# Later layers of two graphs in flight over 29 slots, four graphs to a loop body, four residual additions on TensorE

## The chip, the cores and the metric

The kernel runs on one core of one Trainium2 chip. The metric is the device time of one execution in microseconds. Three runs of the kernel before give a median of 3404.64 us, from 3402.95 to 3406.09.

Engines are named as in the profile: PE (TensorE, matmuls) with PEld (its weight loads), DVE (VectorE), ACT (ScalarE), POOL (GpSimd) and SP (SyncE, which issues every DMA here).

## What is computed

64 graphs of 128 nodes with 128 features go through four graph layers, each followed by a residual and a normalisation. All of it is fp32. Per graph, with `x` and `adj` 128 x 128:

```python
# layer 0: every pair of nodes
h = relu((x @ W1[:H])[:, None] + (x @ W1[H:])[None, :] + b1)   # 128*128 rows of 128
y = layernorm(h @ W2 + b2) * gamma + beta
x = norm(x + einsum('ij,ijh->ih', adj, y))
# layer 1: degree-normalised product, weights, relu; layer 2: two-layer MLP with a node mask
x = norm(x + relu(adj_norm @ x @ W.T + b))
x = norm(x + mask * (relu(((1 + eps) * x + adj.T @ x) @ W1 + b1) @ W2 + b2))
# layer 3: three times
for i in range(3):
    h = relu(layernorm(adj.T @ (h @ Ws[i]) + bs[i] + h) * gammas[i] + betas[i])
x = norm(x + h)
```

Layer 0 is nearly all the arithmetic: 16384 rows per graph. The rest, here called the tail, is a long chain of single 128 x 128 steps.

## The kernel before, in words

A graph's pairs are cut into 16 slots of 8 units (a unit is one node against all 128, a 128 x 128 tile). For slot `t` of a graph:

- `hidden` (DVE L610, ACT L507) makes `h[:, t]` from `uT` and `vT`: DVE 3 units in even slots and 2 in odd ones (`vector_units`), ACT the others. Slots 0 to 13 on ACT read the PSUM copy `v_ps`, 14 and 15 the SBUF copy `vT`.
- `products` (PE L369) multiplies two blocks of 512 columns by `w2c` into one of two PSUM buffers `y_ps`.
- `squares` (ACT L517) squares them into a ring of four, `variances` (PE L381) sums the squares over two slots.
- Each half graph (8 slots), `deviations` (ACT L524) takes the root, SP moves it into another layout (`straighten_deviations`), DVE inverts (L632) and multiplies by the adjacency to the coefficients `c` (L640). SP stores `c` to DRAM and reads it back to all partitions, four broadcasts of 1 MB per half graph (`spread_coefficients`, L305, into `cb`).
- `weighted_sum` (DVE L624) multiplies `h` by `cb` and sums into a column of `gT`: 8 per slot, 128 per graph.

The engines run the same software pipeline, written by hand. An iteration starts one graph and has 16 slots on each engine; a stage of a graph lags by a number of slots: hidden units by START = 4, products by 5, squares by 6, weighted sums by TTR_LAG = 19, the tail by TAIL_LAG = 33. `lagging` turns a lag into a graph and a slot. Each engine's queue is in order, so the order of the work is the order of the program.

The table `AT` gives each tail step a slot and one of FINE = 9 steps in it; on DVE step `k` follows weighted sum `k`. The tail takes 15 slots, so one graph's is in flight at a time, in single buffers. PE does tail steps 0 to 3 between its two products and the others after them; ACT does them between Square and hidden units.

A normalisation is `bn_stats` (L648), `bn_aggr` one step later (L651), two operations on POOL (L848, L850), and NORM_AT = 4 steps after the statistics the scaling on DVE (L657). In layer 3 the residual is added by DVE (L718) from PSUM into `z`, from which statistics and scaling read; layer 0's is L692.

`program` writes out iterations 0 to 3, then a hardware loop `Fori(4, 63)` whose body is one iteration, then four more that drain the pipeline. Inside the loop, waits compare with values worked out from the loop's register.

PE turns `x` of the next graph at slot 14 (`turn_x`, into `turn_bank`), ACT keeps it at the end of slot 15 (`keep_xT`, L489), PE makes `u` and `v` at slot 3 (`make_uv`), ACT keeps them at the end of slot 3 (`keep_uv`, L496 and L497), once per graph. SP's order in an iteration: spread of the first half, output store, `x_in` load, second half's deviations, coefficients and spread, the adjacency load of 8 DMAs, first half's deviations and coefficients, and `load_tail`.

## Time and profile before

| | |
|---|---|
| median of three runs | 3404.64 us |
| profiled execution's own time | 3402.17 us |
| its span, first to last instruction | 3400.4 us |
| PE busy | 2933.5 us (86%), 10882 instructions |
| DVE busy | 2919.2 us (86%), 21905 |
| ACT busy | 2821.7 us (83%), 7620 |
| POOL busy | 403.7 us (12%), 978 |
| mean granted TensorE clock | 0.945 |
| instruction fetch (queue q14) | 318 packets, 2.61 MB |
| chain that ended last | DVE 29%, PE 24%, "issue" 17%, ACT 14% of the span |

"Busy" is the time in which an engine executes something; register, branch, semaphore and DMA-issuing instructions are not in it. "Idle before, releaser" of a row is the time the engine stood before that instruction, and what ended it; "issue" means that nothing the profile shows was waited for. A matmul of fp32 appears as two instructions. The ends of matmuls are modelled, so starts are the safer numbers.

### The profile page before, as it was taken

The page shows a single profiled execution, that of the slowest core. Times are in us where ns is not written, and L with a number is a line of the kernel's source. Part 1 is how long each engine was busy: PE and PEld are TensorE (multiplying, and loading weights), DVE is VectorE, ACT ScalarE, POOL GpSimd, SP SyncE. Part 2 cuts the span into 40 slices and gives each one's busy share as a digit, 9 for nine tenths or more (in the row PEclk, how much of TensorE's full clock was granted, in tenths as well). Part 3 has the DMA queues.
Part 4 walks back from the last instruction along what each step waited for, and adds up shares of the span by engine and source line. Part 5 has one row for each costly group of instructions (what it writes and reads, how often), then busy time and mean ns, then how long its engine had stood idle before and what let it go on. Part 6 is the DMA issues. An engine that isn't in the chain of part 4 may idle for free.

```text
span 3400.4 us, 69689 instructions
## 1 busy us (share of the span) xinstructions
PE 2933.5 (86%) x10882; PEld 1150.1 (34%) x10882; DVE 2919.2 (86%) x21905; ACT 2821.7 (83%) x7620; POOL 403.7 (12%) x978
## 2 busy tenths in 40 slices
PE   8988888888888888888888888888888888888894
PEld 2333333333333333333333333333333333333332
DVE  5988888888888888888888888888888888888896
ACT  8988888888888888888888888888888888888892
POOL 0111111111111111111111111111111111111111
PEclk9999999999999999999999999999999999999996
DMA  3544444444444444444444344444444444434442
GB/s 123 208 159 174 182 167 156 169 191 162 158 171 183 169 156 159 196 167 158 158 181 184 156 159 185 179 159 157 175 190 156 159 175 183 164 156 167 192 162 106
DMA packets 170182, 570.56 MB, mean 168 GB/s; under 512 B 68608, under 2 KB 104320, under 8 KB 104320
## 3 DMA queue, kind: packets, MB, share of 16 engines
q1 hardware_dynamic: 169856, 567.82, 42.8%
q14 instruction: 318, 2.61, 0.2%
q8 instruction: 8, 0.13, 0.0%
HBM read 555.17 MB, written 8.39 MB: 166 GB/s over the span
## 4 chain that ended last, share of the span: by engine, by line
DVE 29%; PE 24%; issue 17%; ACT 14%; SPq 5%; DMA 5%; POOL 4%; DVEq 1%; ACTq 0%; POOLq 0%
PE y_ps L369 14%; DVE h L624 13%; ACT h L507 8%; PE ss_ps L381 6%; DVE h L610 5%; DMA devs<-dev_rows 5%; SPq L286 5%; POOL rs L850 3%; ACT sq L517 2%; DVE gT L624 2%; PE prod_bank L432 2%; ACT dev_rows L524 2%; DVE stats L648 2%; ACT h L555 1%; DVE x L657 1%
## 5 line engine op out<-in xcount | busy, mean ns | idle before, releaser
L369 PE MATMUL y_ps<-h,w2c 128*128 128x512 f32 x4096 | 2152.3, 637 | 209.7 <-DVE h L610 207.1
L624 DVE CUSTOM_DVE_ANT_0 h<-h,cb 128x128 f32<-128x128 f32 x8192 | 1953.1, 283 | 9.4 <-DMA cb<-c_scratch 0.4
L507 ACT ACTIVATE h<-uv_ps,uT 128x128 f32<-128x128 f32 x4928 | 1429.6, 400 | 235.5 <-DVE gT L624 230.3
L517 ACT ACTIVATE sq<-y_ps,b2c_col 128x1024 f32<-128x1024 f32 x1024 | 1164.1, 1137 | 143.8 <-PE y_ps L369 134.9
L369 PEld LDWEIGHTS y_ps<-h,w2c 128*128 128x128 f32 x4096 | 694.7, 196 | 1091.2 <-issue 934.0
L610 DVE TENSOR_SCALAR h<-vT,uT 128x128 f32<-128x128 f32 x2560 | 591.8, 282 | 188.6 <-issue 158.8
L624 DVE DVE_READ_ACCUMULATOR2_ANT gT<- 128x1 f32 x8192 | 670.8, 82 | 0.1
L381 PE MATMUL ss_ps<-sq,sel 128*32 128x512 f32 x4096 | 581.4, 642 | 0.5 <-ACT sq L517 0.5
L848 POOL TENSOR_TENSOR var_eps<-mv,eps_col 128x1 f32<-128x1 f32 x448 | 84.8, 189 | 2657.3 <-DVE mv L651 2657.3
L850 POOL TENSOR_TENSOR rs<-var_eps,minus_half 128x1 f32<-128x1 f32 x448 | 277.0, 618 | 35.1
L507 ACT ACTIVATE h<-vT,uT 128x128 f32<-128x128 f32 x704 | 219.4, 400 | 0.0
L381 PEld LDWEIGHTS ss_ps<-sq,sel 128*32 128x32 f32 x4096 | 82.8, 111 | 351.2 <-issue 297.5
L657 DVE TENSOR_SCALAR x<-z,mv,rs 128x128 f32<-128x128 f32 x256 | 88.7, 346 | 93.3 <-POOL rs L850 91.0
L648 DVE BATCH_NORM_STATS2 stats<-z 128x6 f32<-128x128 f32 x448 | 129.5, 289 | 0.2
L432 PE MATMUL prod_bank<-adj_in,h 128*128 128x128 f32 x256 | 63.7, 331 | 69.2 <-ACT h L555 69.2
L632 DVE RECIPROCAL invs<-devs 128x64 f32<-128x64 f32 x128 | 70.6, 552 | 51.9 <-DMA devs<-dev_rows 47.8
L432 PE MATMUL prod_bank<-adj_in,x 128*128 128x128 f32 x128 | 31.9, 331 | 79.3 <-DVE x L657 79.3
L432 PEld LDWEIGHTS prod_bank<-adj_in,h 128*128 128x128 f32 x256 | 38.9, 191 | 173.4 <-ACT h L555 173.4
L436 PEld LDWEIGHTS prod_bank<-l3w,aggT 128*128 128x128 f32 x384 | 68.9, 194 | 81.4 <-issue 77.4
L555 ACT ACTIVATE h<-z_aff 128x128 f32<-128x128 f32 x192 | 59.5, 310 | 40.5 <-DVE z_aff L731 38.6
L420 PE MATMUL prod_bank<-adj_in,x 128*128 128x128 f32 x128 | 31.9, 331 | 64.0 <-DVE x L657 64.0
L524 ACT ACTIVATE dev_rows<-ss_ps 128x512 f32<-128x512 f32 x128 | 82.6, 645 | 1.2 <-PE ss_ps L381 1.2
(99 smaller groups left out, 1556.2 us busy)
## 6 DMA issues: line engine op xcount, KB each, us to landing
cb<-c_scratch SPq DMA_DIRECT2D x512, 1024.0 KB, 8.1
adj_c<-in_adj_dram SPq DMA_DIRECT2D x512, 8.0 KB
devs<-dev_rows SPq DMA_DIRECT2D x512, 8.0 KB
x_in<-in_x_dram SPq DMA_DIRECT2D x64, 64.0 KB, 9.5
c_scratch<-c SPq DMA_DIRECT2D x128, 32.0 KB, 1.4
adj_in<-in_adj_dram SPq DMA_DIRECT2D x64, 64.0 KB, 2.0
x_res<-in_x_dram SPq DMA_DIRECT2D x64, 64.0 KB, 1.9
out_dram<-x SPq DMA_DIRECT2D x64, 64.0 KB, 10.1
```

The costliest lines, as they stand in the source:

```text
L286: sp.dma_start(devs[32 * p:32 * p + 32, half, :], dev_rows[p:P:32, half, :].rearrange("q (r j) -> q r j", j=SPAN)).then_inc(devs_in[half], 16)
L369: op = pe.matmul(y_ps[:, t % 2, c0:c0 + COLS], w2c[:], h[:, t, c0:c0 + COLS], start=True, stop=True)
L381: mm = pe.matmul(ss_ps[32 * q:32 * q + 32, :], sel[:, ROWS - 1 - p:ROWS - 1 - p + 32], sq[:, (t + q // 2) % SQ_RING, c0:c0 + COLS], start= ...
L432: pe.matmul(prod, (x3 if i == 0 else h3)[:], adj_in[:], start=True, stop=True).then_inc(l3_agged[i], 1)
L507: op = act.activation(h[:, t, n * P:(n + 1) * P], v, ACT.Relu, bias=uT[:, i:i + 1])
L517: act.activation(sq[:, t % SQ_RING, :], y_ps[:, t % 2, :], ACT.Square, bias=b2c_col[:], scale=float(P) ** -0.5).then_inc(sq_done, 1)
L524: act.activation(dev_rows[:, half, :], ss_ps[:], ACT.Sqrt, bias=EPS).then_inc(dev_done, 1)
L610: op = dve.tensor_scalar(h[:, t, n * P:(n + 1) * P], vT[:], uT[:, i:i + 1], 0.0, ALU.add, ALU.max)
L624: op = dve.tensor_tensor_reduce(h[:, t, cols], h[:, t, cols], cb[:, t // 2, c0:c0 + P], 1.0, 0.0, ALU.mult, ALU.add, gT[:, i:i + 1])
L648: dve.bn_stats(stats[:], z[:]).then_inc(stats_set[name], 1)
L657: dve.tensor_scalar(dst[:], z[:], mv[:, 0:1], rs[:], ALU.subtract, ALU.mult).then_inc(normed[name], 1)
L850: pool.tensor_tensor(rs[:], var_eps[:], minus_half[:], ALU.pow).then_inc(rs_set[name], 1)
```

## The change

- **Two tails in flight.** The tail's steps are placed over 29 slots (the last, `ln3`, at slot 28). `tails` gives two graphs with their buffers to every engine at every slot, one in its first 16 slots, one in its last. All tail tensors get a second buffer, and there are two PSUM product banks; the bank of the transposes goes, its parts move into `prod_bank` and `uv_ps`.
- **Four graphs to a loop body** (UNROLL): seven iterations are written out, 56 are done in 14 rounds of four, and four drain.
- **Four residual additions** (`l0_sum` and `l3_sum0` to `2`) become a third product into the same PSUM sum, identity by residual. `bn_stats`, layer 3's first scaling (`z_aff`) and layer 0's normalisation then read PSUM.
- NORM_AT is 7 for both scalings. `norm`'s order is otherwise the same.
- **DVE makes 2 hidden units in every slot**, ACT 6. `uT` and `vT` have two buffers. ACT reads `v_ps` up to slot 12 (SPLIT_AT).
- Weighted sums and tail start one slot earlier (18 and 32). DVE does its hidden units after the first weighted sum of a slot.
- The transpose of `x` moves to slot 1, `make_uv` to slot 2, `keep_xT` to the end of slot 1, `keep_uv` into slot 3 behind the Square. SP loads the tail after the adjacency and stores the output after that.

```diff
-TTR_LAG = START + 15
-TAIL_LAG = START + 29
+TTR_LAG = START + 14
+TAIL_LAG = START + 28
+UNROLL = 4
+SPLIT_AT = 13
-NORM_AT, AFFINE_AT = 4, 5
+NORM_AT = 7
-def vector_units(t):
-    return 3 if t % 2 == 0 else 2
+VECTOR_UNITS = 2
...
+    ("g_keep", 2, 0), ("l0_mm", 3, 0), ("ln0", 3, 4), ("x1_scaled", 4, 5),
...
+    ("l3_agg0", 12, 4), ("l3_agg_keep0", 13, 2), ("l3_mm0", 13, 4),     ("l3_ln0", 14, 3), ("l3_relu0", 16, 2), ("l3_agg1", 19, 0), ("l3_agg_keep1", 19, 8),
...
-            for i in range(4):
-                iteration(i + 1, (i, *(i - d if i >= d else None for d in range(1, 4))))
-            with eng.Fori(4, G - 1) as g:
-                iteration(g + 1, (g, g - 1, g - 2, g - 3))
+            first = 4 + (G - 5) % UNROLL
+            for i in range(first):
+                iteration(i + 1, about(i), i % 2)
+            with eng.Fori(0, (G - 1 - first) // UNROLL) as rounds:
+                for n in range(UNROLL):
+                    g = UNROLL * rounds + (first + n)
+                    iteration(g + 1, (g, g - 1, g - 2, g - 3), (first + n) % 2)
...
+        def tails(graphs, buf, s):
+
+            return [(graphs[d], (buf - d) % 2, (s + SLOTS * (d - 2)) * FINE) for d in (2, 3)]
...
-                    pe.matmul(prod, gT_keep[:], w2cg[:], start=True, stop=False)
-                    pe.matmul(prod, adjT[:], beta0[:], start=False, stop=True).then_inc(l0_made, 1)
+                    pe.matmul(out, gT_keep[:, b, :], w2cg[:], start=True, stop=False)
+                    pe.matmul(out, adjT[:, b, :], beta0[:], start=False, stop=False)
+                    pe.matmul(out, ident[:], x_base[:, b, :], start=False, stop=True).then_inc(l0_made, 1)
...
+                        pe.matmul(out, aggT[:, b, :], l3w[:, i, :], start=True, stop=False)
+                        pe.matmul(out, ident[:], (x3 if i == 0 else h3)[:, b, :], start=False, stop=False)
+                        pe.matmul(out, pick[:], bias_parts[:, 1 + i, :], start=False, stop=True
...
+                    if s == 1 and new is not None:
+                        turn_x(new)
+                    if s == 2 and new is not None:
+                        make_uv(new)
...
-                    for n in range(first, DUO_UNITS):
-                        if n == first + 2:
-                            later_layers(g, place + 4, place + 6)
+                    for n in range(VECTOR_UNITS, DUO_UNITS):
+                        if n == VECTOR_UNITS + 2:
+                            tail_steps(4, 6)
...
+                    if s == 1 and new is not None:
+                        keep_xT(new)
...
-                    if due(f"l3_sum{i}"):
-                        wait(dve, l3_made[i], g + 1)
-                        dve.tensor_tensor(z[:], prod, (x3 if i == 0 else h3)[:], ALU.add).then_inc(z_set[name], 1)
...
-                    hidden_step = BLOCK_UNITS if ht == 0 else 0
+                    hidden_step = BLOCK_UNITS if ht == 0 else 0 if t == 0 else 1
```

## Rows read from the trace of the kernel before

**Rows 1.** All executions of line L497: count, duration min/median/max, first and last start.
```profile
L497 ACT ACTIVATE vT<-uv_ps x64: 267/268/271, 11.0 to 3281.4; 128x128 f32<-128x128 f32 x64
```

**Rows 2.** Timeline of ACT, L497 of graphs 3 and 4: start, duration.
```profile
142.62 0.27 ACT L497 ACTIVATE vT<-uv_ps 128x128 f32<-128x128 f32 x1
...
190.88 0.27 ACT L497 ACTIVATE vT<-uv_ps 128x128 f32<-128x128 f32 x1
```

**Rows 3.** Busy by stretch: length, PE, PEld, DVE, ACT, POOL, PEclk, DMA share, GB/s.
```profile
53.60:95.60 42.00, 40.33 (x142) 12.77 (x140) 38.41 (x307) 41.37 (x111) 0.85 (x3) 1.00 0.52 203
...
142.90:191.20 48.30, 43.80 (x174) 17.07 (x170) 45.18 (x344) 43.95 (x120) 6.13 (x15) 1.00 0.46 182
191.20:243.70 52.50, 45.54 (x178) 17.77 (x170) 45.88 (x346) 44.09 (x120) 6.20 (x15) 0.97 0.47 184
```

**Rows 4.** Waits from 243.7 to 3281: us in total, times, longest.
```profile
ACT h L507 <- DVE gT L624: 224.0, 80, 4.1
...
DVE h L610 <- issue: 156.0, 57, 2.9
...
ACT sq L517 <- PE y_ps L369: 127.3, 194, 2.3
...
DVE x L657 <- POOL rs L850: 79.8, 174, 0.5
...
ACT aggT L542 <- PE prod_bank L421: 66.0, 58, 1.4
DVE z L718 <- PE prod_bank L437: 60.2, 174, 0.5
```

**Rows 5.** Timeline over one end of the loop's body: start, duration, [idle before].
```profile
1644.62 1.14 ACT L517 ACTIVATE sq<-y_ps,b2c_col 128x1024 f32<-128x1024 f32 x1
...
1648.89 0.68 DVE L610 TENSOR_SCALAR h<-vT,uT 128x128 f32<-128x128 f32 x3 [2.80 <-issue]
...
1649.69 1.65 PE L369 MATMUL y_ps<-h,w2c 128*128 128x512 f32 x2 [3.50 <-DVE h L610]
...
1652.23 1.14 ACT L507 ACTIVATE h<-uv_ps,uT 128x128 f32<-128x128 f32 x4 [3.91 <-DVE gT L624]
```

**Rows 6.** Timeline of ACT in a stretch where it is the bound.
```profile
51.08 1.85 ACT L507 ACTIVATE h<-vT,uT 128x128 f32<-128x128 f32 x6
...
55.71 1.17 ACT L517 ACTIVATE sq<-y_ps,b2c_col 128x1024 f32<-128x1024 f32 x1
56.70 1.72 ACT L507 ACTIVATE h<-uv_ps,uT 128x128 f32<-128x128 f32 x6
58.20 1.23 ACT L517 ACTIVATE sq<-y_ps,b2c_col 128x1024 f32<-128x1024 f32 x1
```

**Rows 7.** Groups by line: count | busy us, mean ns | idle before.
```profile
L610 DVE TENSOR_SCALAR h<-vT,uT 128x128 f32<-128x128 f32 x2560 | 591.8, 282 | 188.6 <-issue 158.8 <-ACT vT L497 4.0 <-ACT mask_all L562 3.1
...
L731 DVE SCALAR_TENSOR_TENSOR z_aff<-z_aff,rs,l3beta 128x128 f32<-128x128 f32 x192 | 66.7, 347 | 2.6 <-POOL rs L850 2.6
...
L718 DVE TENSOR_TENSOR z<-prod_bank,h 128x128 f32<-128x128 f32 x128 | 37.3, 291 | 37.5 <-PE prod_bank L437 37.5
...
L701 DVE SCALAR_TENSOR_TENSOR z_aff<-prod_bank,dis,l1b 128x128 f32<-128x128 f32 x64 | 22.2, 347 | 2.0 <-PE prod_bank L417 2.0
```

**Rows 8.** Timeline of PE, an identity product and the product behind it.
```profile
152.34 0.39 PE L421 MATMUL prod_bank<-ident_eps,x 128*128 128x128 f32 x2
152.56 1.02 PE L369 MATMUL y_ps<-h,w2c 128*128 128x512 f32 x2
```

**Rows 9.** Timeline of DVE and SP, from the coefficients to their broadcast.
```profile
1645.02 0.23 DVE L640 CUSTOM_DVE_ANT_0 c<-adj_c,invs 128x64 f32<-128x64 f32 x1
...
1647.68 2.00 SPq L305 DMA_DIRECT2D cb<-c_scratch  x4
```

**Rows 10.** Tile `cb` from 1590 to 1660, twelve broadcasts of 1 MB.
```profile
DMA to landing us min/median/max: 4.4/7.8/12.2
```

**Rows 11.** Line L688 from 3300 to 3401, the last two graphs.
```profile
L688 DVE COPY gT_keep<-gT x2: 221/224/226, 3327.5 to 3367.6; 128x128 f32<-128x128 f32 x2
```

More of the change, by code:

```diff
@@ L333, in iteration @@
                         load_adj_c(new)
+                    load_tail(old, 1 - buf)
+                if oldest is not None:
+                    wait_apart(sp, normed["ln3"], oldest + 1)
+                    wait_apart(sp, out_stored, 16 * oldest)
+                    sp.dma_start(out[oldest], x4[:, 1 - buf, :]).then_inc(out_stored, 16)
                 if new is not None:
@@ L336, in iteration @@
                     store_coefficients(new, 0)
-                if old is not None:
-                    load_tail(old)
             program(sp, iteration)
@@ L347, in turn_x @@
                 wait(pe, x_in_in, 16 * (g + 1))
-                wait(pe, adjT_set, g - 2)
-                wait(pe, xT_set, g)
+                wait(pe, uv_ready, g)
+                wait(pe, h_act, SLOTS * (g - 1) + SPLIT_AT)
                 pe.transpose(xturn_ps, x_in[:], ident[:]).then_inc(x_turned, 1)
@@ L459, in _, with iteration @@
             pe.wait_ge(set_up, 1)
-            def iteration(after, graphs):
+            def iteration(after, graphs, buf):
                 new = graphs[0]
@@ L559, in later_set_up, with iteration @@
                 act.wait_ge(wT_turned, 1)
-                act.activation(l1wT[:], prod, ACT.Copy).then_inc(wT_set, 1)
+                act.activation(l1wT[:], prod[0], ACT.Copy).then_inc(wT_set, 1)
                 act.wait_ge(mask_turned, 1)
-                act.activation(mask_all[:], turn_ps[:, 0:G], ACT.Copy).then_inc(mask_set, 1)
+                act.activation(mask_all[:], prod[1][:, 0:G], ACT.Copy).then_inc(mask_set, 1)
             act.wait_ge(weights_in, 16 * WEIGHTS)
-            keep_xT(0)
             act.wait_ge(b2c_set, 1)
-            def iteration(after, graphs):
+            def iteration(after, graphs, buf):
                 new = graphs[0]
@@ L686, in later_layers @@
                     wait(dve, ttr_done, SLOTS * (g + 1))
-                    wait(dve, l0_made, g)
-                    dve.tensor_copy(gT_keep[:], gT[:]).then_inc(g_kept, 1)
-                if due("l0_sum"):
-                    wait(dve, l0_made, g + 1)
-                    wait(dve, x_base_set, g + 1)
-                    dve.tensor_tensor(z[:], prod, x_base[:], ALU.add).then_inc(z_set["ln0"], 1)
-                norm(g, "ln0", x1, lo, hi)
+                    wait(dve, l0_made, g - 1)
+                    dve.tensor_copy(gT_keep[:, b, :], gT[:]).then_inc(g_kept, 1)
+                norm(g, b, "ln0", x1, lo, hi)
                 if due("x1_scaled"):
@@ L778, in later_set_up, with iteration @@
                 dve.wait_ge(affine_set, 2)
-            def iteration(after, graphs):
+            def iteration(after, graphs, buf):
                 new = graphs[0]
@@ L792, in iteration @@
                             if hg is not None:
-                                for n in range(vector_units(ht)):
-                                    hidden(hg, ht, n)
+                                for n in range(VECTOR_UNITS):
+                                    hidden(hg, hb, ht, n)
                         elif wg is not None:
                             weighted_sum(wg, t, k - (k > hidden_step))
-                        later_layers(g, place * FINE + k, place * FINE + k + 1)
+                        for g, b, place in tails(graphs, buf, s):
+                            later_layers(g, b, place + k, place + k + 1)
                         if ct % HALF == 0 and cg is not None and k == 5:
@@ L847, in later_layers, with iteration @@
                         wait(pool, mv_set[name], g + 1)
[L848 removed]
+                        pool.tensor_tensor(var_eps[:, b:b + 1], mv[:, b, 1:2], eps_col[:], ALU.add
+                                           ).then_inc(eps_added[name], 1)
                         wait(pool, eps_added[name], g + 1)
[L850 removed]
+                        pool.tensor_tensor(rs[:, b:b + 1], var_eps[:, b:b + 1], minus_half[:], ALU.pow
+                                           ).then_inc(rs_set[name], 1)
             pool.wait_ge(ones_set, 5)
[L854 removed]
+            def iteration(after, graphs, buf):
                 for s in range(SLOTS):
[L856 to L857 removed]
+                    for k in range(FINE):
+                        for g, b, place in tails(graphs, buf, s):
+                            later_layers(g, b, place + k, place + k + 1)
             program(pool, iteration)
```

272 lines of the change are left out of this document (131 added, 141 removed), and 15 rows, old and new, of the table AT.

## Prediction, made before the changed kernel was run

> **What bounds the kernel now.** I read the views in this order: the whole iterations, the waits of the loop, one passage over the end of the loop body, the pitch of single instructions.
>
> First the length of an iteration. ACT's copy of `vT` (L497) runs once per graph and marks time. Graph 3's starts at 142.62 and graph 4's at 190.88: 48.26 us, in the last iteration written out ahead of the loop, with the pipeline full. Graph 63's starts at 3281.4, so the 59 iterations in the loop took (3281.4 - 190.88) / 59 = 52.38 us each [rows 1, 2]. The loop body has the same work and costs 4.12 us more, 243 us in all.
>
> Then who is full. In the written-out iteration DVE is busy for 45.18 us, ACT 43.95, PE 43.80. DVE is the first bound and the others are close. In the iteration from 53.6 to 95.6, before any tail runs, ACT is busy for 41.37 of 42.00 us, 98.5%: ACT as the bound leaves almost no gap [rows 3].
>
> Then the loop's 4.12 us. Of the waits inside it, DVE's hidden unit waits 156.0 us for "issue", 57 times: 2.74 us once per iteration. The passage over the body's end shows it: DVE starts L610 at 1648.89 after 2.80 us of nothing, PE after 3.50 us (for that DVE result), ACT later still, 3.91 us for `gT`. ACT's own turn into the next iteration, the Square at 1644.62, has no gap listed before it: ACT wrapped round at no cost and stood only because DVE did [rows 4, 5]. Behind the gap PE runs two products in 1.65 us, against 1.02 elsewhere; the granted clock is 1.00 in the written-out iteration and 0.97 in the first looped one [rows 3, 5, 8]. So an end of the body costs 2.74 us of fetch on DVE and some 1.4 us behind it.
>
> **The change, part by part, per full iteration.**
>
> Four graphs to a body. The first seven iterations are written out, 56 stay in the loop: 14 rounds, 13 jumps back instead of 58. At (243 / 58) = 4.19 us a jump, 45 fewer give -189 us. The cover of the 13 that stay goes down: ACT will have no spare time (below), so I keep the full 4.19.
>
> The rule of the Trainium skill that bears on this is in "Runtime: NRT & Kernel Launch", section "Instruction fetch mechanics": a taken branch to a target outside the two held blocks (512 instructions, 2048 on PE) forces a fetch before execution goes on. The trace agrees as far as DVE stalls and ACT, with a third of the instructions, does not. By that rule the fourfold bodies of ACT, SyncE and GpSimd no longer fit either, which is a rival below.
>
> Hidden units. DVE makes 2 of 8 in each slot, not 3 and 2 by turns: 8 units move to ACT. On ACT a slot of Square and six hidden units is 58.20 - 55.71 = 2.49 us, the six being (58.20 - 56.70) / 6 = 0.25 each: +2.0 us. Six more units read `vT` in SBUF (SPLIT_AT 13 instead of 14); six from there take 1.85 us against 1.72, so +0.1 [rows 6]. ACT: 43.95 + 2.1 = 46.1 us busy. DVE loses 8 x 0.231 (591.8 / 2560) = 1.85 us [rows 7].
>
> Four residual additions. DVE loses four of 0.29 us (37.3 / 128) = 1.2 us, 0.8 if their overlap with neighbours is left out; I take 1.0. PE gains four fp32 identity products; the one that exists, L421, starts at 152.34 and the next product at 152.56: 0.22 each, +0.9 us, of which no part is the bound. Statistics and scaling now read PSUM. An operation that does so already, L701, takes 347 ns, the same form from SBUF, L731, 347: nothing, at most 0.07 x 9 = 0.6 us on DVE if each were worse by a fifth, none of it on the path while DVE has the room below [rows 7, 8].
>
> Sums per full iteration: ACT 46.1, PE 43.8 + 0.9 = 44.7, DVE 45.2 - 1.85 - 1.0 = 42.3.
>
> Waits. A tail that takes 29 slots gives each step about twice the distance to its source. In the loop that can free DVE of POOL's `rs` (79.8 us, 1.4 per iteration) and of PE's product (60.2, 1.0), and ACT of PE (L542: 66.0, 1.1) [rows 4]. I do not add these, since the sum is made from ACT's busy time. NORM_AT 7 puts six weighted sums ahead of the normalisation, so DVE no longer stands there. What is late next is ACT itself: it is in order, and Square, hidden units and tail steps fill it. New waits: `keep_xT` now ends ACT's slot 1 and needs PE's transpose from the same slot; behind it on ACT stands the next Square, which PE's next but one product needs. Ahead of that transpose PE has two products of 1.02 us [rows 8] and the small ones of c_sum, some 2.5 us of a 2.9 us slot, so I price it at 0 to 0.5 us. On the SyncE queue the `x_in` load waits for that same transpose ahead of `straighten_deviations(old, 1)`; that one is due at slot 6, so nothing. The store of the output has moved behind the tail's loads and is ready by slot 13, one slot before the deviations behind it: nothing.
>
> The length: ACT 46.1 at 98.5% gives 46.8; with the `keep_xT` wait and a PE at 95% beside it I take 47.0 (bounds 46.1 and 48.3). That is 48.3 - 47.0 = 1.3 us less per iteration.
>
> Weighted sums one slot earlier. The broadcast of coefficients has one slot less. `c` is made at 1645.02, its spread issued at 1647.68, and the first landing is 4.4 us after issue at best: 1652.1, 7.1 us after `c` [rows 9, 10]. From slot 15, step 6, to slot 18 are 2.3 slots of 2.94 us = 6.8 us. So DVE may stand for 0.3 us, twice per iteration, in a spare of 47.0 - 42.3 = 4.7 us: nothing in the sum. In exchange ACT's hidden units come two slots behind the sums that free `h`, which is the wait of 224.0 us of the loop [rows 4].
>
> Fill and drain. Iterations 0 and 1 are ACT's: +2 us each; 2 and 3 gain 1.3 each: +1.4. At the end the last `gT_keep` starts at 3367.6 and the span ends at 3400.4 [rows 11]: 32.8 us of pure chain, in which four additions (4 x 0.29) leave and four products at half clock (4 x 0.44) come; graph 62's second half now runs beside it in the same in-order queues. I take +3 (bounds 0 and +10).
>
> **Sum.** Against the profiled execution's 3402.17: -189 - 59 x 1.3 (77) + 1.4 + 3 = 3140.6. The median of the runs is 2.5 us above that execution: 3143.
>
> **Rivals.**
>
> (a) The loop's extra time is not the jump alone. If only 2.74 us belong to the jump and the other 1.45 us to each looped iteration (waits on register values, which every looped iteration keeps), then (45 - 3) x 1.45 = 61 us don't go: 3204. For it: a wait in the loop compares with a value worked out from the loop's register, in a written-out iteration with a constant. Against it: behind the gap PE is visibly slow, and ACT's longest waits for `gT` stand there [rows 4, 5]. Chance 0.18.
>
> (b) PE and ACT hold each other. PE at 44.7 and ACT at 46.1 share two y buffers; in the loop ACT's Square already waits 127.3 us for PE [rows 4]. If their jitter costs what DVE's relief gives, the iteration stays at 48.3: 3143 + 77 = 3220. Against it: those waits fall mostly behind the gap, and the iteration at 98.5% had the same buffers. Chance 0.17.
>
> (c) Every engine fetches at the jump. ACT's own 2.8 us come on top of the DVE chain, 13 x 2.8 = 36: 3179. This is what the rule named above would add, if the engines' fetches do not overlap. Chance 0.15, within reach of the forecast.
>
> (d) ACT runs without a gap at 46.1 and a jump costs only DVE's 2.74 us: -53 - 19: 3071. Chance 0.07.
>
> (e) Slower. The broadcast decides. If with the earlier sums each half comes as late as its slowest landing (12.2 us instead of 4.4, [rows 10]), DVE stands 8.1 us twice, 16.2 less the spare 4.7: +11.5 per iteration, 3143 + 63 x 11.5 = 3870. It beats the 259 us gained from 4.4 us per full iteration on, that is when each half is late by some 4.5 us. Against it: the later landings belong to later pieces, each needed two slots after the one before. Chance 0.03.
>
> **How the numbers follow.** The forecast, 3143 (3110 to 3175 by its own bounds), has 0.39. It is the likeliest, so it is the number. For 8 in 10 the range takes in (a), (b) and (c) and reaches two thirds of the way to (d): 3090 to 3235. The last 0.01 is for an outcome near no change. A difference from no change can be told for this kernel from about 0.2%, 7 us. Faster by more than that: 0.96; within it 0.01; slower 0.03.
>
> **What would show it.** Right: `vT` copies in the loop about 47 us apart with one of about 51 in four; DVE's "issue" wait 13 times, not 57; ACT busy for over 93% of the middle; DVE with idle time of 3 to 5 us per iteration, mostly at the reciprocal and the first weighted sums. (a): evenly 48.4 in the loop's straight parts, with ACT below 96% busy. (b): ACT's Square waiting for PE for over 1 us per iteration. (c): an "issue" wait on ACT. (e): L624 waiting for the DMA of `cb`. Wrong altogether if written-out iterations come to more than 48.3 us.

## The result, and the profile after

The changed kernel takes 3042.06 us, the median of four runs from 3027.88 to 3046.78. Beside it on the same chip the kernel before takes 3405.36. The ratio is 0.8925, 95% interval 0.8894 to 0.8956: 363 us less, where 262 were forecast, and below the range's lower end of 3090. The profiled execution of after took 3046.78 us, its span is 3045.0.

The lines of the page of after that matter: span, busy time by engine, the granted clock in 40 slices, instruction fetch, the chain that ended last, and ACT's two large groups.

```profile
span 3045.0 us, 67885 instructions
...
PE 2900.1 (95%) x11394; PEld 1178.0 (39%) x11394; DVE 2679.4 (88%) x21137; ACT 2883.4 (95%) x8132; POOL 424.1 (14%) x978
...
PEclk9999999999999999999999999999999999999996
...
q14 instruction: 408, 3.34, 0.3%
...
ACT 67%; issue 14%; PE 8%; DMA 7%; DVE 2%; SPq 2%; ACTq 0%; POOL 0%; DVEq 0%; POOLq 0%
...
L512 ACT ACTIVATE h<-uv_ps,uT 128x128 f32<-128x128 f32 x4992 | 1739.5, 776 | 0.0
...
L522 ACT ACTIVATE sq<-y_ps,b2c_col 128x1024 f32<-128x1024 f32 x1024 | 1560.1, 1524 | 29.6 <-PE y_ps L375 29.5
```

ACT holds 67% of the chain, and the pieces of 0.2 to 1.0 us that the chain calls "issue" between 2470 and 2530 us all lie between two instructions of ACT, not at a jump. One group to note: a hidden unit on ACT has a mean of 776 ns and a Square 1524. The same Square took 1.17 and 1.23 us where ACT stood now and then [rows 6]. That has to do with the error of the forecast.

Then three iterations in a row inside the loop: two undisturbed ones and one that holds a jump back. Columns: stretch, length, PE, PEld, DVE, ACT and POOL busy, PEclk, DMA share, GB/s. They answer to [rows 3].

```profile
2424.48:2469.07 44.59, 44.17 (x178) 17.63 (x177) 41.67 (x329) 44.59 (x129) 6.32 (x15) 1.00 0.50 198
2469.07:2513.94 44.87, 44.32 (x180) 17.91 (x180) 41.18 (x327) 44.87 (x129) 6.61 (x15) 1.00 0.50 194
2513.94:2566.36 52.42, 48.56 (x178) 19.49 (x178) 43.46 (x344) 45.76 (x130) 6.56 (x15) 0.90 0.54 212
```

The first two take 44.6 and 44.9 us with ACT busy throughout, and so do those written out ahead of the loop (44.86 or 44.87 for graphs 3 to 5); that an iteration waits on a loop's register makes no difference. The one with the jump takes 52.42, at a mean clock of 0.90. The iteration right behind a jump, not shown, takes 45.8 on average.

The 13 iterations with a jump have not one price: four take 49.0 to 49.5 us at a mean clock of 0.965, eight 52.0 to 52.8 at 0.902, and the first 55.0 at 0.907. DVE stands 2.7 to 3.0 us in both kinds, PE 3.3 to 3.8 in the first and 3.3 to 4.5 in the second; what differs is how much of the iteration PE runs at the lower clock.

The waits of after (us in total, times, longest), against [rows 4]:

```profile
DVE invs L639 <- DMA devs<-dev_rows: 126.1, 108, 26.8
DVE h L631 <- DMA cb<-c_scratch: 107.5, 113, 3.6
PE y_ps L375 <- DVE h L617: 73.0, 69, 4.5
ACT xT L494 <- PE uv_ps L358: 55.5, 13, 5.4
DVE h L631 <- issue: 36.6, 13, 3.0
...
ACT sq L522 <- PE y_ps L375: 29.5, 27, 2.2
```

ACT's wait for `gT` (224.0 before) is gone and its wait for PE is 29.5 instead of 127.3. DVE stops for "issue" 13 times instead of 57, 2.8 us each. In its place come a wait of ACT for PE's transpose, 4.3 us 13 times, and DVE's waits for transfers, which lie in the time that DVE has spare.

**Where the 94 us between forecast (3140.6) and the profiled execution are.** `vT` of graph 4 starts at 187.39, that of graph 63 at 2930.93: 2743.5 us for 59 iterations.

| Term | forecast | measured | difference |
|---|---|---|---|
| undisturbed iteration, x59 | 47.0 | 44.87 | -126 |
| 13 jumps | 54.5 | 2743.5 - 59 x 44.87 = 96 (7.4 each) | +42 |
| up to graph 4 | 190.88 + 1.4 = 192.3 | 187.39 | -5 |
| behind graph 63's `vT` | 119.0 + 3 = 122 | 3045.0 - 2930.93 = 114.1 | -8 |

That is -97; the other 3 us are the rounding of 48.26 to 48.3 in the forecast's gain of 1.3 per iteration. Two terms have to be explained, an iteration that is shorter and a jump that is dearer, and they have opposite signs.

### The profile page after: what moved, and what is told of

The parts are those of the page before. It is cut to its first block, busy times and chain, and to the rows that moved or that the text cites. A ratio compares the mean times of both kernels' runs of the same rounds, so it can differ in the third digit from the quotient of the medians.

```text
span 3045.0 us, 67885 instructions
## 1 busy us (share of the span) xinstructions
PE 2900.1 (95%) x11394; PEld 1178.0 (39%) x11394; DVE 2679.4 (88%) x21137; ACT 2883.4 (95%) x8132; POOL 424.1 (14%) x978
## 4 chain that ended last, share of the span: by engine, by line
ACT 67%; issue 14%; PE 8%; DMA 7%; DVE 2%; SPq 2%; ACTq 0%; POOL 0%; DVEq 0%; POOLq 0%
ACT h L512 37%; ACT sq L522 22%; PE y_ps L375 5%; DMA cb<-c_scratch 3%; ACT dev_rows L529 2%; ACT aggT L555 2%; DMA devs<-dev_rows 2%; SPq L295 2%; PE ss_ps L387 1%; ACT aggT L547 1%; DMA c_scratch<-c 1%; DVE h L631 1%; ACT h L560 0%; ACTq L208 0%; ACT xT L494 0%
## 5 line engine op out<-in xcount | busy, mean ns | idle before, releaser
L631 DVE CUSTOM_DVE_ANT_0 h<-h,cb 128x128 f32<-128x128 f32 x8192 | 1936.8, 281 | 146.2 <-DMA cb<-c_scratch 107.5
L512 ACT ACTIVATE h<-uv_ps,uT 128x128 f32<-128x128 f32 x4992 | 1739.5, 776 | 0.0
L522 ACT ACTIVATE sq<-y_ps,b2c_col 128x1024 f32<-128x1024 f32 x1024 | 1560.1, 1524 | 29.6 <-PE y_ps L375 29.5
L617 DVE TENSOR_SCALAR h<-vT,uT 128x128 f32<-128x128 f32 x2048 | 485.6, 279 | 8.3 <-ACT vT L502 4.3
L512 ACT ACTIVATE h<-vT,uT 128x128 f32<-128x128 f32 x1152 | 446.0, 870 | 0.0
L560 ACT ACTIVATE h<-z_aff 128x128 f32<-128x128 f32 x192 | 129.4, 674 | 27.8 <-DVE z_aff L742 27.6
L555 ACT ACTIVATE aggT<-prod_bank 128x128 f32<-128x128 f32 x192 | 134.0, 698 | 19.7 <-PE prod_bank L436 19.7
L665 DVE BATCH_NORM_STATS2 stats<-prod_bank 128x6 f32<-128x128 f32 x256 | 74.8, 292 | 41.4 <-PE prod_bank L415 34.9
L494 ACT ACTIVATE xT<-uv_ps 128x128 f32<-128x128 f32 x64 | 45.0, 703 | 55.5 <-PE uv_ps L358 55.5
L440 PE MATMUL prod_bank<-l3w,aggT 128*128 128x128 f32 x384 | 81.1, 294 | 4.2 <-ACT aggT L555 2.6
L668 DVE BATCH_NORM_AGGREGATE mv<-stats 128x2 f32<-128x6 f32 x448 | 78.3, 175 | 0.3
```

The source lines that it names most:

```text
L440: pe.matmul(out, aggT[:, b, :], l3w[:, i, :], start=True, stop=False)
L512: op = act.activation(h[:, t, n * P:(n + 1) * P], v, ACT.Relu, bias=uT[:, b, i:i + 1])
L522: act.activation(sq[:, t % SQ_RING, :], y_ps[:, t % 2, :], ACT.Square, bias=b2c_col[:], scale=float(P) ** -0.5).then_inc(sq_done, 1)
L555: act.activation(aggT[:, b, :], prod[b], ACT.Copy).then_inc(l3_agg_kept[i], 1)
L560: act.activation(h3[:, b, :], z_aff[:, b, :], ACT.Relu).then_inc(l3_relued[i], 1)
L617: op = dve.tensor_scalar(h[:, t, n * P:(n + 1) * P], vT[:, b, :], uT[:, b, i:i + 1], 0.0, ALU.add, ALU.max)
```

## The experiments

Theory A: ACT is the bound of an undisturbed iteration, and its iteration is the sum of the distances from start to start of its instructions, not of their durations. A jump costs DVE's fetch and, behind it, PE at half clock, which ACT then waits for. Rival B: the iteration is held by the coupling of PE and ACT over two `y` buffers, so that work taken off ACT brings nothing. Rival C: the extra time of the loop is not the jump alone.

Results in one table; "from" is the kernel that was edited. "Iteration" is the mean from one `vT` copy to the next between graphs 4 and 63, those with a jump left out; "with a jump" is the mean of these. In the text an undisturbed iteration is the usual one, 44.87 us in after and e1; their means are higher by some longer ones. The runs stand on several chips, on which the kernel before took from 3402.89 to 3408.47 us, so differences between runs of different chips are good to some 5 us.

| Run | from | median us | ratio to before (95%) | iteration | with a jump |
|---|---|---|---|---|---|
| after | | 3042.06 | 0.8925 (0.8894 to 0.8956) | 45.07 | 51.57 |
| e1_all_written_out | after | 2958.06 | 0.8691 (0.8676 to 0.8705) | 44.95 | |
| e2_two_to_a_body | after | 3139.89 | 0.9222 (0.9203 to 0.9241) | 45.66 | 50.95 |
| e4_adds_on_dve | after | 3022.65 | 0.8892 (0.8862 to 0.8922) | 45.12 | 49.65 |
| e8_pe_kept_busy | after | 2998.62 | 0.8811 (0.8796 to 0.8826) | 45.06 | 47.86 |
| e3_units_3_2 | after | 3015.94 | 0.8871 (0.8846 to 0.8897) | 44.99 | 49.59 |
| e7_out_units_2_1 | e1 | 3086.94 | 0.9069 (0.9051 to 0.9087) | 47.06 | |
| e5_out_units_3_2 | e1 | 2929.01 | 0.8594 (0.8578 to 0.8610) | 44.61 | |
| e12_out_units_3_every_4 | e1 | 2914.12 | 0.8551 (0.8536 to 0.8565) | 44.33 | |
| e11_out_keep_same_slot | e1 | 2953.19 | 0.8666 (0.8651 to 0.8680) | 44.89 | |
| e14_out_chain_in_one_slot | e1 | 3012.99 | 0.8851 (0.8836 to 0.8866) | 45.85 | |
| e6_before_four | before | 3270.44 | 0.9599 (0.9583 to 0.9615) | 48.45 | 56.31 |
| e13_before_four_padded | e6 | 3229.54 | 0.9486 (0.9470 to 0.9502) | 48.42 | 53.25 |
| e9_before_written_out | before | 3152.48 | 0.9261 (0.9243 to 0.9280) | 48.13 | |
| e10_before_out_units_2 | e9 | 3091.04 | 0.9081 (0.9063 to 0.9099) | 47.09 | |

### What a jump costs

**No jump at all.**

```diff
-            first = 4 + (G - 5) % UNROLL
-            for i in range(first):
+            for i in range(G - 1):
                 iteration(i + 1, about(i), i % 2)
-            with eng.Fori(0, (G - 1 - first) // UNROLL) as rounds:
-                for n in range(UNROLL):
...
```

> The changed kernel with all 67 iterations written out, no loop and no jump; everything else as it is. In the changed kernel the iterations inside a round take 44.6 to 45.9 us between two vT copies and the one over a jump up to 52.4. Theory A (a jump costs 7.4 us in all: 2.8 of fetch on VectorE, the rest in TensorE at half its clock behind the gap): 13 jumps go, 3042 - 96 = 2946 us, and the granted clock comes to 1.00 outside fill and drain. Rival B (a jump costs the 4.19 us of the prediction and the rest of the loop's excess has another cause): 2988. Rival C (looped iterations are dear because their waits use register values): every one of 56 iterations gains, and the written-out kernel's iterations come out shorter than the 44.86 us of graphs 3 to 6.

2958.06, 84 us less than after: 84 / 13 = 6.5 us a jump (7.4 in the slower profiled execution). It lies between A's 2946 and B's 2988, nearer to A. The undisturbed iteration stays at 44.87, so looped iterations are not dear by themselves.

**Twice as many jumps**: `UNROLL = 2`, 28 jumps.

> The changed kernel with two graphs to a body instead of four: 5 iterations written out, 29 rounds, 28 jumps instead of 13. Theory A (7.4 us a jump): 3042 + 15 x 7.4 = 3153 us. Rival B (4.19 us a jump, as in the prediction): 3105. Rival D (a smaller body is fetched in less time or not at all on ACT, PE and SyncE): under 3080.

3139.89: (3139.89 - 3042.06) / 15 = 6.5 us for each added jump, between A's 7.4 and B's 4.19. That this equals the 6.5 of after is not a law of the jump: this body stops DVE twice per jump, 2.8 us and, starting 0.9 us later, 4.1, together 6.9 instead of 2.8. So part of the two stops must be covered; how much each costs was not isolated. The waits (us in total, times, longest):

```profile
DVE gT L631 <- issue: 116.1, 28, 4.6
...
DVE h L631 <- issue: 78.9, 28, 3.0
```

**Inside one jump of after** (start, duration, idle before). DVE stops 2.79 us; PE then takes 3.77 and 3.48 us for two slots' products. A product of 512 columns appears as two instructions, so each `x4` is two products, at some 1.8 us each against 1.02 [rows 8]. ACT stands twice behind PE.

```profile
2366.47 0.29 DVE L631 CUSTOM_DVE_ANT_0 h<-h,cb 128x128 f32<-128x128 f32 x1 [2.79 <-issue]
...
2367.29 3.77 PE L375 MATMUL y_ps<-h,w2c 128*128 128x512 f32 x4 [3.54 <-DVE h L617]
...
2371.57 0.45 PE L358 MATMUL uv_ps<-ident,x_in 128*128 128x128 f32 x1
...
2372.14 0.28 ACT L494 ACTIVATE xT<-uv_ps 128x128 f32<-128x128 f32 x1 [4.40 <-PE uv_ps L358]
...
2373.82 3.48 PE L375 MATMUL y_ps<-h,w2c 128*128 128x512 f32 x4
...
2377.34 1.11 ACT L522 ACTIVATE sq<-y_ps,b2c_col 128x1024 f32<-128x1024 f32 x1 [2.17 <-PE y_ps L375]
```

The stretch in numbers, columns as above; the granted clock is 0.53, the 1.2 GHz level nearly throughout, where the 10 us before it had 1.00. PE had just stood for 3.54 us.

```profile
2366.00:2376.00 10.00, 8.71 (x20) 3.73 (x21) 8.61 (x70) 4.77 (x15) 0.66 (x1) 0.53 0.86 336
```

The transpose that ACT's `keep_xT` waits for stands behind two products at that clock. ACT's two stops at this jump come to 4.40 + 2.17 = 6.6 us; the mean cost of a jump in this execution is 7.4.

**PE kept at work over DVE's stop.** Four products whose result is overwritten, ahead of the first real one of each body, on an `h` slot that has long been made (work added, outputs unchanged).

```diff
+                    if s == 0 and at_jump[0]:
+                        wait(pe, sq_done, SLOTS * yg + t - 1)
+                        for _ in range(4):
+                            pe.matmul(y_ps[:, t % 2, 0:COLS], w2c[:], h[:, t - 1, 0:COLS], start=True, stop=True)
```

> The changed kernel with four extra products of 512 columns (about 3.6 us) on PE at the head of each round of the loop, into the y buffer that the next product overwrites: they fill the gap in which PE waits for VectorE after the jump. They add work and no result. Theory A (some 4 of a jump's 7 us are PE at half its clock behind the gap): the granted clock stays at 1.00 over the jump, the iteration over a jump falls from 49 to 52 to about 48, and the time by 13 x 3.5 = 45 us: 2997. Rival B (the clock is a symptom, what costs is the order of the queues): 3042 within 10. Rival C (the extra products only delay PE): 13 x 3.6 = 47 us slower, 3089.

2998.62, 43 us less than after, as A expected (2997). Each iteration with a jump takes 47.9 instead of 49.0 to 55.0. The four extra products are the eight instructions of the first line, and the real one behind them (two instructions) runs at full speed:

```profile
498.46 3.70 PE L478 MATMUL y_ps<-h,w2c 128*128 128x512 f32 x8
502.00 1.02 PE L379 MATMUL y_ps<-h,w2c 128*128 128x512 f32 x2
```

ACT's wait for the transpose of `x` is gone from the waits (one for that of `adj`, 29.6 us in 14, stands there instead), and DVE's stop is as it was, 35.5 us in 13. So of 84 us of jumps half (43) is PE's clock, and the other 41 (3.1 per jump) is what DVE's stop of 2.8 costs with PE at full speed.

**The four additions back on DVE.**

```diff
-                    pe.matmul(out, ident[:], x_base[:, b, :], start=False, stop=True).then_inc(l0_made, 1)
...
+                    dve.tensor_tensor(z[:, b, :], prod[b], x_base[:, b, :], ALU.add).then_inc(z_set[name], 1)
...
-                        pe.matmul(out, ident[:], (x3 if i == 0 else h3)[:, b, :], start=False, stop=False)
...
+                    dve.tensor_tensor(z[:, b, :], prod[b], res[:, b, :], ALU.add).then_inc(z_set[name], 1)
```

> The changed kernel with the four residual additions back on VectorE, right ahead of the statistics, without the identity products. Theory A (ACT sets the iteration, VectorE has 3 us of room and PE some): nothing, 3042 within 10 us, and the span of an undisturbed iteration stays at 44.86. Rival B (PE is the bound beside ACT): 4 x 0.22 us less on PE, 59 x 0.9 = 53 us faster, 2990. Rival C (VectorE's work stands in a path): 4 x 0.2 us more, 3090.

3022.65, 19 us less than after and outside A's 10, though the two intervals (0.8862 to 0.8922, 0.8894 to 0.8956) overlap. The iterations without a jump are the same, 45.1 on average in both. So the identity products, which the change names, bring nothing here: DVE, which they relieve, isn't the bound. The 19 us lie in the jumps: 11 of 13 at 48.9 to 49.5 us (clock 0.965) and two at 52.2 (0.902), where the profiled execution of after has four and eight (and the 55.0). But each kernel also has a run of the other kind: after one of 3027.88 us at a clock of 0.979, e4 one of 3040.14 at 0.974. So it isn't shown that the four products per graph on PE make a jump dearer; which of the two prices a jump gets varies from run to run.

### What bounds the undisturbed iteration

**One unit in two slots taken from DVE and given to ACT** (from e1; ACT +8 units per graph), and **one in two slots given back to DVE**, written out and in the loop.

```diff
-VECTOR_UNITS = 2
+def vector_units(t):
+    return 2 if t % 2 == 0 else 1      # e7;  3 and 2 in e5 and e3
```

> The changed kernel, written out, with VectorE making 2 and 1 hidden units by turns: 8 units per graph more on ACT. The written-out changed kernel takes 2958 us and 44.97 per iteration. Theory A (ACT is the bound by the pitch of its instructions, 0.25 us a unit): +2.0 per graph, 2958 + 63 x 2.0 = 3084 us. Rival B (ACT still has room behind PE): under 3050. Rival C (units from ACT's queue delay PE as well): over 3110.

3086.94, and the undisturbed iteration goes from 44.87 to 46.99: +2.1 for eight units of 0.25. ACT is the bound, with no slack at all.

> The changed kernel, written out, with 3 and 2 hidden units on VectorE by turns. Written out it takes 2958 us; in the loop the same edit of the units gave 26 us. Theory A (the three engines are then equally full, 43.3 to 43.6 us of 44.7 busy, and their jitter eats most of it): 44.5 per iteration, 2935. Rival B (the 26 us came from the jumps, where ACT has less to catch up): 2955 or more. Rival C (ACT was the only bound and the jumps hid the gain): 2958 - 63 x 1.6 = 2857.

2929.01, 0.3 us less per iteration, from 44.95 on average to 44.6, where 2 us were taken off ACT. Now no engine is the bound alone. Written out, the stretch from 200 to 2800 of e1, then of e5:

```profile
200.00:2800.00 2600.00, 2562.24 (x10298) 1040.82 (x10295) 2400.28 (x19094) 2596.29 (x7346) 381.66 (x866) 1.00 0.51 199
```

```profile
200.00:2800.00 2600.00, 2523.42 (x10368) 1067.16 (x10367) 2504.01 (x19702) 2518.76 (x6938) 382.90 (x876) 1.00 0.52 200
```

ACT goes from 99.9% to 96.9%, DVE from 92.3 to 96.3, PE from 98.5 to 97.1: three engines within a per cent of each other, none full.

The timelines of ACT tell more than the busy shares. Give each instruction the distance to the next start that it has in e1's unbroken stretches: Square 1.00, a unit 0.25 from PSUM and 0.29 from SBUF, `dev_rows` 0.48, a copy 0.16, `hid` and `uT` 0.25, a relu 0.20. What an iteration takes above that sum is ACT waiting, listed as idle or not (means over 56 iterations):

| Run | iteration | sum of distances | above it | of this ahead of Squares |
|---|---|---|---|---|
| e7 | 47.06 | 46.10 | 0.96 | 0.62 |
| e1 | 44.96 | 44.02 | 0.94 | 0.51 |
| e12 | 44.33 | 43.02 | 1.31 | 0.74 |
| e5 | 44.61 | 41.97 | 2.64 | 1.72 |

With 1.5 and 2 units on DVE the iteration is ACT's sum and an unchanged 0.95; with 2.5 the Squares wait for PE. So B's coupling exists, but as the next limit behind ACT's.

> The changed kernel with VectorE making 3 and 2 hidden units by turns again, so ACT has 8 units of 0.25 us less per graph. Theory A (ACT alone sets the 44.86 us of an undisturbed iteration, by the pitch of its instructions): the iteration falls towards the next engine, VectorE at 41.5 + 1.85 = 43.3 us busy: 43.4 to 43.9, time 2960 to 2990. Rival B (PE, 44.3 us busy of 44.7, is as much the bound): the iteration stays above 44.5, 3020 to 3045. Rival C (VectorE's delays at the coefficients then decide): slower, above 3050.

3015.94, 26 us less than after, where A expected 52 to 82: nearer to B. In the loop the gain lies elsewhere than in e5: the iterations without a jump take 44.99 on average, after's 45.07, and those with one 49.6 instead of 51.6. As with e4, part of that may be which price the jumps got in this execution.

**Three units in every fourth slot** (from e1: `return 3 if t % 4 == 0 else 2`).

> The changed kernel, written out, with 3 hidden units on VectorE in every fourth slot and 2 in the others: 4 units per graph from ACT to VectorE. Theory A (ACT is the bound until about 44.4 us): 4 x 0.25 = 1.0 off until the others bind, 44.3 per iteration: 2920 to 2935, at or under the version with 3 and 2 by turns. Rival B (what that version gains is all there is, in proportion): 2945.

2914.12, below A's 2920 to 2935, with an iteration of 44.3 us: the best of all, 128 us below after and 491 below before. Of the four splits tried, 1.5, 2, 2.25 and 2.5 units, the third is the best.

### What the staging over 29 slots brings

**The old kernel written out, then with 2 units per slot.** e9 replaces the loop of before by 63 iterations in a row; e10 also has `vector_units` return 2.

> The kernel before with all its iterations written out and nothing else changed. Its last written-out iteration took 48.26 us against 52.38 in the loop. Theory A (the whole excess of 4.1 us belongs to the jump): 190.9 + 59 x 48.3 + 119 + 2 = 3160 us, 245 less than before. Rival B (some of the excess belongs to the jump only, and late iterations have another load than the fourth): 3200 or more.

3152.48, a little under A's 3160, beside 3402.89 for before on that chip: 250.4 / 58 = 4.32 us a jump, against the 4.19 that the prediction read from the trace.

> The kernel before, written out, with VectorE making 2 hidden units in every slot, so 8 units per graph move to ACT; one tail at a time and the additions on VectorE as before. Theory A (VectorE, its work and its 2.9 us of waits for POOL and PE, sets the 48.3 us; ACT's pitch comes to 44.9): 48.3 - 1.85 = 46.4, which is 118 us under the written-out kernel before: about 3040. Rival B (ACT already the bound at 46.8, as the prediction had it): 3070. Rival C (the waits of the tail vanish once VectorE has room, so that two tails in flight bring nothing): 44.9 per iteration, 2960.

3091.04, an iteration of 47.07: every expectation was missed. With the units shared as in e1, the old staging, and whatever else the change moves, costs 2.1 us more per iteration. The waits of e10 from 200 to 2800 show ACT late at one copy per graph and at one Square, and DVE at three sums:

```profile
DVE z L716 <- PE prod_bank L435: 89.4, 165, 0.7
...
ACT aggT L540 <- PE prod_bank L419: 37.7, 56, 0.7
...
ACT sq L515 <- PE y_ps L367: 22.5, 55, 0.5
```

Their listed part on ACT is (37.7 + 22.5) / 55 = 1.1 us. The rest lies under the overlap of ACT's records, and the distances from start to start show it: e10's iteration of 47.08 is a sum of 43.76 and 3.32 above it, e1's 44.02 and 0.94. So the whole 2.1 us is ACT coming late to work that others have to finish first: in e10 1.0 ahead of Squares, 0.9 at that copy, 0.6 ahead of hidden units, 0.3 at the relus, 0.3 at `uT` and 0.2 at the other copy. Which part of the change (two tails, `make_uv` earlier, the weighted sums' lag) removes which was isolated for the copy alone, below.

**Part of the old closeness put back into the new kernel** (from e1): each step one slot or less behind its source.

```diff
-NORM_AT = 7
+NORM_AT = 4
...
-    ("ln1", 7, 2), ("l2_agg", 8, 4), ("l2_agg_keep", 9, 2),
+    ("ln1", 8, 0), ("l2_agg", 8, 4), ("l2_agg_keep", 8, 8),
```

> The changed kernel, written out (2958 us), with layer 1's normalisation, layer 2's product and its copy on ACT in one slot as in the kernel before: NORM_AT 4, ln1 at (8, 0), the copy at (8, 8). Theory A (what two tails bring to an ACT-bound iteration is that no source is late for ACT; in the kernel before with 2 units these waits add up to 2.1 us per graph, 0.8 of it at this copy): +0.8 per graph, 3010 us, with a wait of ACT for PE at the copy of about 0.7 us. Rival B (the distance within the slot is enough, and the 2.1 us come from the single buffers and the lag of the weighted sums): under 2970, no such wait.

3012.99, as A expected (3010): +0.95 us per iteration. On ACT a single listed wait comes with it, the copy of the aggregate behind PE, 57 times between 200 and 2800 us:

```profile
ACT aggT L542 <- PE prod_bank L420: 54.6, 57, 1.3
```

The copy moved alone, e11 (`("l2_agg_keep", 8, 8)` and no more), costs nothing: 2953.19, as B expected.

> The changed kernel, written out, with one tail step of ACT back in the place it had: the copy of layer 2's aggregate at the end of the slot of its product (8, 8) instead of one slot later (9, 2). Theory A (what two tails in flight bring is the distance of ACT's steps from their sources: in the kernel before with 2 units, this copy waits 0.68 us per graph by the profile and some 0.15 more under the end of the instruction before it): +0.8 per graph, 2958 + 50 = 3008 us. Rival B (ACT makes it up elsewhere): 2958 within 8.

So the distance to a source counts only as a whole: with step, normalisation and copy in one slot ACT is late by 1 us; with the normalisation earlier no wait at the copy is listed. (e14's `NORM_AT` of 4 holds for every normalisation; on DVE it brings waits for POOL, 118.8 us in 256 at `x`, in time that DVE has spare.)

### The old kernel's jumps, four times fewer

**Four iterations to a body in the kernel before**, nothing else.

```diff
-            with eng.Fori(4, G - 1) as g:
-                iteration(g + 1, (g, g - 1, g - 2, g - 3))
+            with eng.Fori(0, 14) as rounds:
+                for n in range(4):
+                    g = 4 * rounds + (7 + n)
+                    iteration(g + 1, (g, g - 1, g - 2, g - 3))
```

> The kernel before with four graphs to a loop body and nothing else of the change: 7 iterations written out, 13 jumps instead of 58. The kernel before takes 3404 us in the loop and 3152 written out, 252 / 58 = 4.34 us a jump. Theory A (a jump of the old schedule costs the same at 13 as at 58): 3152 + 13 x 4.34 = 3209 us; the prediction's own term (189 less) says 3215. Rival B (a jump of the fourfold body costs the 6.5 us that it costs in the changed kernel, because now PE, ACT and SyncE fetch too): 3152 + 85 = 3237.

3270.44: 135 us less than before where 196 (A) or 168 (B) was expected, so neither holds: (3270.4 - 3152.5) / 13 = 9.1 us a jump. DVE stops twice, 2.55 us apart, and PE stands 6.63 us:

```profile
2337.61 0.29 DVE L612 TENSOR_SCALAR h<-vT,uT 128x128 f32<-128x128 f32 x1 [2.95 <-issue]
2340.16 0.48 DVE L612 TENSOR_SCALAR h<-vT,uT 128x128 f32<-128x128 f32 x2 [2.26 <-issue]
...
2340.78 2.07 PE L371 MATMUL y_ps<-h,w2c 128*128 128x512 f32 x2 [6.63 <-DVE h L612]
```

**The same, with 64 instructions of 1 column put on DVE ahead of the loop**, so that the loop's head lies elsewhere in the instruction stream.

```diff
+            if eng is engines.get("dve"):
+                for k in range(64):
+                    eng.memset(pad[:, k:k + 1], 0.0)
```

> The kernel before with four graphs to a body (3270 us), and 64 small memsets of a scratch tile on VectorE ahead of the loop; they cost 4 to 9 us once and do nothing else but move the head of VectorE's loop by 64 instructions. In that kernel VectorE stands at issue twice at each jump, 26 times in all, 2.95 us before its first hidden unit and 2.26 us right after it. Theory A (a second block of instructions begins just behind the loop's head, and is fetched only when the first is there): the second stop goes, 13 times instead of 26, and with what follows it 30 to 50 us: 3225 to 3245. Rival B (a longer body makes a jump dearer by itself, wherever its head lies): 3272 to 3280, still 26 times.

3229.54, 41 us less for 64 instructions more, as A expected (3225 to 3245). The stops fall from 26 to 13; the first line is e6's, the second e13's:

```profile
DVE h L612 <- issue: 63.2, 26, 3.0
```

```profile
DVE h L618 <- issue: 36.0, 13, 3.1
```

One hidden unit of DVE runs between the two stops of e6, and moving the loop's head takes the second one away, so it reads as a second fetch right behind the head. The Trainium skill, "Runtime: NRT & Kernel Launch", section "Instruction fetch mechanics", says that instructions come in blocks of 256 and that a branch out of the two blocks held forces a fetch; a head close ahead of a block's end would give just this, and the padding's effect agrees. The Trainium skill calls the crossing of a block's end mostly hidden; right behind a jump it was not: the second stops of e6 take 2.0 to 2.3 us, the first ones 2.7 to 3.0.

Of the 13 jumps left, each costs (3229.5 - 3152.5) / 13 = 5.9 us. Part of that isn't the iteration with the jump: the others in the loop take 48.42 us on average against 48.13 written out. Whether that is the loop's register or the aftermath of the jumps was not isolated.

## Why the prediction was wrong, point by point

- **"ACT 46.1 at 98.5% gives 46.8", taken as 47.0: the step that failed**, worth -126 us. The mechanism (ACT becomes the bound) was right; the term was made from ACT's busy time, and busy time is not work. The prediction left the waits for the tail out of its sum, "since the sum is made from ACT's busy time"; but part of ACT's waits was inside that time: by the distances from start to start ACT's work in an iteration of the old kernel is 41.7 us (e9), where the prediction took 43.95 busy. A stretch of e1's ACT in which no idle time is listed:

```profile
1002.75 0.58 ACT L539 ACTIVATE aggT<-prod_bank 128x128 f32<-128x128 f32 x1
1002.90 1.43 ACT L517 ACTIVATE sq<-y_ps,b2c_col 128x1024 f32<-128x1024 f32 x1
...
1022.86 1.01 ACT L550 ACTIVATE aggT<-prod_bank 128x128 f32<-128x128 f32 x1
1023.02 2.40 ACT L507 ACTIVATE h<-uv_ps,uT 128x128 f32<-128x128 f32 x6
1024.52 1.91 ACT L517 ACTIVATE sq<-y_ps,b2c_col 128x1024 f32<-128x1024 f32 x1
```

  A copy of the same form is recorded with 0.58 and 20 us later with 1.01 us, but the next instruction starts 0.15 to 0.16 us behind it both times. In this stretch a recorded duration reaches past the start of the next instruction, by more the longer ACT has not stood, and waits shorter than this overlap count as busy. From start to start, an iteration of after (2469.07 to 2513.94) is: 16 Squares of 1.00, 13 x 6 units from PSUM in 1.50, 3 x 6 from SBUF in 1.75, two `dev_rows` of 0.485, and 2.4 for the nine copies, `hid` and the three relus: 16.0 + 19.5 + 5.25 + 0.97 + 2.4 = 44.1. The other 0.75 us are stops too short to be listed. The prediction had the rows for most of it: it took 2.49 us for a slot of Square and six units by starts [rows 6], but only for the difference, and added it to a busy time of 43.95. By starts alone, 16 x 2.49 = 39.8, the 3.4 us of the other instructions and 0.75 for three slots from SBUF (both as the trace of after has them) come to 44.0. What the prediction's 47.0 does match is e10 with 47.1, two units a slot on the old staging. The 2.1 us that the change's new staging takes off from there are waits that the busy time held.
  The Trainium skill, "ScalarE: Activation LUTs", section "What ACT_TABLE_LOAD costs", has consecutive ACTIVATEs overlap by about 93 ns. Here the recorded overlap is 0.12 us where ACT has just stood (`vT` at 2378.61 of after: 0.28 recorded, 0.16 to the next start), near to that, and 0.85 in an unbroken stretch, which is not.
- **"I keep the full 4.19" per jump: mis-sized**, 6.5 us by the medians, 7.4 in the profiled execution, +42 us in that. That the cover goes down was said; its size wasn't worked out. DVE's stop is as predicted, 2.8. What was sized wrongly is `keep_xT`, "0 to 0.5 us": at full clock no such wait is listed (e1), but behind a stop PE runs at half of it, and two of its products at some 1.8 us lie ahead of the transpose. The wait measured 4.3 us, 13 times. (The prediction's "two products in 1.65 us, against 1.02" is one product, in its two instructions.) The price came from a kernel in which ACT waited 6.4 us per iteration (e9) and could make up for a delay; that this is what made the jump dearer is argued, not shown, since the old kernel too paid 5.9 a jump with four graphs to a body (e13).
- **Additions**: +0.9 us on PE and -1.0 on DVE, neither on the path: right for the undisturbed iteration (e4: no change). At the jumps no effect is shown.
- **PSUM as a source**, "at most a fifth": right. `x` from PSUM takes 402 ns, from SBUF 338, 19% more; the statistics 292 against 286; the first step of the layer 3 scaling, L737, 345 as the SBUF form L742.

```profile
L675 DVE TENSOR_SCALAR x<-z,mv,rs 128x128 f32<-128x128 f32 x192 | 64.9, 338 | 4.0 <-POOL rs L863 3.9
...
L675 DVE TENSOR_SCALAR x<-prod_bank,mv,rs 128x128 f32<-128x128 f32 x64 | 25.7, 402 | 0.9 <-POOL rs L863 0.9
```

- **Weighted sums a slot earlier**, 0.3 us twice, hidden: about 1 us each (107.5 us in 113 waits), three times the forecast, and hidden all the same, since DVE has 44.87 - 41.18 = 3.7 us spare. Rival (e) did not occur.
- **Fill and drain**: +4.4 forecast, 5 and 8 us less than that measured. The fill is mostly the shorter iteration again: from graph 2 to 4 it takes 43.8 and 44.9 us instead of 47.3 and 48.3; the drain wasn't traced further.
- **Rival (a)** is refuted for the new kernel: a looped iteration takes 44.59 to 44.87, a written-out one 44.87. In the old kernel 0.3 us per iteration are seen (48.42 against 48.13), a fifth of what (a) needed. **Rival (b)** is refuted as the bound by e7, and is the next one by e5. **Rival (c)** did not occur: no "issue" wait on ACT. The prediction had ACT, SyncE and GpSimd among the engines whose fourfold body no longer fits; by the size that it names this holds for ACT alone, since the trace of after lists 701 instructions of ACT in four iterations, 428 of SyncE and 72 of GpSimd. A fetch of ACT that ended while it stood for PE's transpose would show in no view. **Rival (d)** had the iteration right in direction (46.1), not in size, and the jump wrong.
- **The range** had its lower end two thirds of the way to (d). It took ACT's busy time as a floor, and all of its width went to costs above it. The two errors, -126 and +42 us, had opposite signs, so it was luck that the forecast came out no further off.

The 363 us by parts, from the medians of runs on several chips: all jumps of the old kernel gone, -253 (3405 to 3152, e9); two units a slot, -61 (e10: 3091); two tails in flight, with the rest of the change, -133 (e1: 2958); the 13 jumps of the new body, +84: 3042. The fourfold body by itself would have brought 135 of it to the old kernel (e6), 176 with its loop's head in a better place (e13).

## What to carry to other kernels

Where an engine is nearly full, add up the distances from start to start of its instructions; the recorded durations overlap, and a busy share of 98% can hide several per cent of waiting. The price of a stall doesn't carry over from one loop body to another: here it was 4.3, 5.9, 6.5 and 9.1 us a jump. Where a stall stops PE, the half clock behind it has to be put through each wait of the slots that follow. An engine that a change relieves matters only if it is the bound: here the additions on TensorE brought nothing, while shifting one unit in four slots was worth 44 us (2958 to 2914).

## What the runs showed of the hardware

- ACT's recorded duration of a 128-column copy grows from 0.28 us behind a stop (`vT` at 2378.61 of after) to 1.01 us in a stretch without one (e1), with 0.15 to 0.16 us to the next start in both.
- A unit on ACT that reads SBUF takes 1.75 / 6 = 0.29 us from start to start, from PSUM 1.50 / 6 = 0.25. The forecast had 0.1 us for six more from SBUF; it is 0.25.
- DVE's stop behind a jump is 2.6 to 3.1 us, and where a second follows, it is 2.0 to 2.3 in e6 and 116.1 / 28 = 4.1 in e2 (13 stops in after, 56 in e2's 28 jumps, 26 in e6, 13 in e13). In the old kernel 64 idle instructions ahead of the loop removed one of two stops and 41 us.
- In the new kernel half of a jump's cost was the TensorE clock, and jumps came at two prices by it: 49.0 to 49.5 us for the iteration at a mean clock of 0.965, 52.0 to 52.8 at 0.902. Four products without a use, run during DVE's stop, kept the granted clock at 0.99 over the whole run instead of 0.97 and gave back 43 us.
